# A three-layer graph convolution on one core: nine dense tiles in layer 0 instead of eight, and a new order for the end of that layer

## The reference, cut to what matters

```python
def _gcn_conv(x, W, b, src, dst, norm, n_nodes):
    xw = x @ W
    msg = xw[src] * norm[:, None]
    out = jax.ops.segment_sum(msg, dst, num_segments=n_nodes)
    return out + b
...
src, dst, norm = _gcn_norm(edge_index, n)     # 6250 nodes, 106250 edges sorted by dst, then self loops again
h = _gcn_conv(x, W1, b1, src, dst, norm, n)
h = _gcn_conv(h, W2, b2, src, dst, norm, n)
h = _gcn_conv(h, W3, b3, src, dst, norm, n)
return _layernorm(x + h, axis=-1)
```

## Time and profile before

| | us |
|---|---|
| median of 3 runs | 2347.21 (2343.35 to 2349.53) |
| the profiled execution's own time | 2344.56 |
| its span | 2342.7 |
| PE busy | 2024.8 (86%) |
| POOL busy | 1611.0 (69%) |
| DVE busy | 1490.5 (64%) |
| ACT busy | 803.4 (34%) |

### The profile page before, as it was taken

How to read it: one execution, slowest core, us unless ns; L and a number is a source line. 1 busy time by engine, 2 the same in 40 slices (tenths; PEclk the granted TensorE clock), 3 DMA queues, 4 the chain that set the end, 5 groups by cost and what they waited for, 6 DMA issues and landing times.

```text
span 2342.7 us, 32832 instructions
## 1 busy us (share of the span) xinstructions
PE 2024.8 (86%) x10242; PEld 1157.4 (49%) x10242; DVE 1490.5 (64%) x3665; ACT 803.4 (34%) x1521; POOL 1611.0 (69%) x1698
## 2 busy tenths in 40 slices
PE   6655777899989988779999999998899999999764
PEld 6321223454445433246666566664466666666431
DVE  8435776777767764355555555556656666666787
ACT  0602553444434433233333333334333333323110
POOL 0257777777777777647777777777577777777760
PEclk7766899999999998999999999999899999999876
DMA  8556888888888888758888888889688888898883
GB/s 281 211 167 181 277 271 249 249 251 248 245 254 286 277 253 249 232 159 243 249 248 250 258 269 269 266 264 320 200 242 262 262 260 280 273 287 285 282 279 113
DMA packets 288153, 585.68 MB, mean 250 GB/s; under 512 B 73204, under 2 KB 132529, under 8 KB 287985
## 3 DMA queue, kind: packets, MB, share of 16 engines
q0 software_dynamic: 132784, 434.04, 60.9%
q1 hardware_dynamic: 155200, 149.59, 19.3%
HBM read 516.40 MB, written 67.06 MB: 249 GB/s over the span
## 4 chain that ended last, share of the span: by engine, by line
PE 34%; POOL 12%; issue 6%; DVE 2%; DMA 2%; ACT 0%; DVEq 0%; ACTq 0%
PE ps L1299 25%; POOL ring L972 12%; PE ps L1186 7%; PE ps L1197 1%; DMA ring<-y_dram,kept 1%; PE ps L1198 1%; DVE acc L2115 0%; PE ps L1354 0%; DVE ln L1973 0%; DMA out_dram<-row_sb 0%; DVE acc L1918 0%; DMA onehot<-a_dram 0%; DVEq L1914 0%; DVE y_words L1964 0%; DVE y_words L1971 0%
## 5 line engine op out<-in xcount | busy, mean ns | idle before, releaser
L972 POOL DMA_INDIRECT ring<-y_dram,kept x1650 | 1582.4, 959 | 588.0 <-issue 492.3
L1186 PE MATMUL ps<-ring,onehot 128*32 128x512 f32 x3300 | 467.7, 634 | 80.0 <-DMA ring<-y_dram,kept 78.7
L2115 DVE SCALAR_TENSOR_TENSOR acc<-ps,acc 128x512 f32<-128x512 f32 x494 | 341.1, 690 | 277.7 <-PE ps L1299 261.6
L1299 PE MATMUL ps<-dense_first,wide_a 128*128 128x512 f32 x1144 | 321.3, 402 | 14.0 <-DVE dense_first L2086 6.4
L1299 PEld LDWEIGHTS ps<-dense_first,wide_a 128*128 128x128 f32 x1144 | 213.8, 191 | 103.7 <-issue 26.7
L1299 PE MATMUL ps<-dense_next,wide_a 128*128 128x512 f32 x820 | 238.6, 399 | 8.0 <-ACT wide_a L1542 6.7
L1542 ACT CAST wide_a<-onehot 128x512 fp32r<-128x512 uint8 (+1 forms) x297 | 171.3, 593 | 202.4 <-PE ps L1299 124.2
L1918 DVE SCALAR_TENSOR_TENSOR acc<-ps,mask,acc 128x512 f32 x280 | 197.2, 746 | 67.9 <-issue 65.7
L1299 PE MATMUL ps<-dense_first,y_rows 128*128 128x512 f32 x756 | 211.7, 401 | 2.5 <-DVE dense_next L2086 1.7
L1885 DVE TENSOR_TENSOR onehot<-ps,kept 128x128 f32<-128x128 f32 x417 | 119.4, 287 | 145.6 <-PE ps L1186 143.2
L1503 ACT CAST ring<-ps 128x490 uint8<-128x490 f32 x228 | 154.2, 692 | 138.9 <-PE ps L1256 137.4
(11 more groups left out here) (289 smaller groups left out, 2302.7 us busy)
## 6 DMA issues: line engine op xcount, KB each, us to landing
onehot<-a_dram SPq DMA_DIRECT2D x456, 64.0 KB
ring<-y_dram,kept POOLq DMA_INDIRECT x1650, 4.1
y_dram<-acc SPq DMA_DIRECT2D x99, 256.0 KB, 10.1
a_dram<-ring SPq DMA_DIRECT2D x19, 784.0 KB, 6.0
acc<-in_x_dram SPq DMA_DIRECT2D x1, 12288.0 KB
y_dram<-acc SPq DMA_DIRECT2D x12, 1024.0 KB, 11.0
out_dram<-row_sb SPq DMA_DIRECT2D x48, 256.0 KB
w_sb<-in_x_dram SPq DMA_DIRECT2D x24, 256.0 KB, 4.0
```

Of the source, the lines that this page charges most:

```text
L972: pool.indirect_dma_start(ring[:, s, :], None, y_dram[layer], bass.IndirectOffsetOnAxis(ap=rows, axis=0)).then_inc(done, 16)
L1186: mm = pe.matmul(ps[k * WIDE:(k + 1) * WIDE, g % BANKS, :], wide_hot[:, r, k, :], ring[:, r * CPQ + k, :], start=opens, stop=closes, tile_ ...
L1299: mm = pe.matmul(ps[:, bank, :], wide_slots[n % WIDE_SLOTS][:, P * k:P * (k + 1)], y_parts[(TILES * (layer - 1) + tile) % YSLOTS][:, part, :],
L2115: dve.scalar_tensor_tensor(out=rows, in0=ps[:, UNIT_BANKS[n % len(UNIT_BANKS)], :], scalar=0.5, in1=rows, op0=ALU.mult, op1=ALU.add).then_ ...
```

## The change

`EARLY_DENSE` goes from 8 to 9. One more tile of destinations in layer 0 is then dense, its sparse groups begin one group later, and there are 25 more units. `EARLY_END = 16` sets where the units end, 22 quads ahead of the layer's end instead of 30. The remaining windows end with the units (`REST_QUADS`), before `LATE_AT`. From `LATE_AT` on, finished tiles may come in consecutive quads, and their products go into the bank in which windows were built (`BUILD_BANK`), so that a turn need not wait for the bias of the tile before.

```diff
-EARLY_DENSE = 8
+EARLY_DENSE = 9
+EARLY_END = 16
...
-    REST_QUADS = LAYER_QUADS[0] - REST_AT - 6
...
-    UNITS0_TO = LAYER_QUADS[0] - 6 - 3 * EARLY_DENSE
+    UNITS0_TO = LAYER_QUADS[0] - 6 - EARLY_END
+    REST_QUADS = UNITS0_TO - REST_AT
+    LATE_AT = UNITS0_TO + 2
...
-            at = max(q, at + 2)
+            at = max(q, at + (1 if at >= LATE_AT else 2))
...
+    def late_turn(turn):
+        return FINISH[0][turn][0] >= LATE_AT
...
                 if turn > 0:
                     pe.wait_ge(turn_copied, turn)
-                    pe.wait_ge(h_ready, turn)
+                    if not late_turn(turn - 1):
+                        pe.wait_ge(h_ready, turn)
...
                     for t in finished_at(0, q):
-                        multiply_tile(TURN_OF[0][t], TURN_BANK)
+                        if late_turn(TURN_OF[0][t]):
+                            pe.wait_ge(win_kept, WINDOWS)
+                        multiply_tile(TURN_OF[0][t], BUILD_BANK if late_turn(TURN_OF[0][t]) else TURN_BANK)
...
                     for t in finished_at(0, q):
-                        bias_rows(0, t, h_sb, TURN_BANK, TURN_OF[0][t])
+                        bias_rows(0, t, h_sb, BUILD_BANK if late_turn(TURN_OF[0][t]) else TURN_BANK, TURN_OF[0][t])
```

More of the change, by code:

```diff
@@ L270, in gcn_three_layers_resnorm @@
     assert all(q < LAYER_QUADS[layer] for layer in range(LAYERS) for q, late, t in FINISH[layer])
-    assert all(abs(a[0] - b[0]) > 1 for a, b in zip(FINISH[0], FINISH[0][1:])) and len(pair_of(0)) == PAIR and Y0_SLOTS == 2 * PAIR
+    assert all(b[0] - a[0] > (0 if a[0] >= LATE_AT else 1) for a, b in zip(FINISH[0], FINISH[0][1:])) and window_quad(WINDOWS - 1) < LATE_AT and len(pair_of(0)) == PAIR and Y0_SLOTS == 2 * PAIR
     assert all(len(windows_at(q)) <= WIDE0_SLOTS for q in UNIT0_QUAD) and REST_AT + 2 < UNITS0_FROM and (TILES - 1) % PAIR == 0
```

## The result

| | before | after |
|---|---|---|
| median | 2346.75 us (11 executions, 2341.73 to 2353.21) | 2355.64 us (11 executions, from 2351.85) |
| ratio, 95% interval | | 1.0036 [1.002, 1.0051] |
| the profiled execution, its span | 2344.56, 2342.7 | 2352.24, 2350.4 |

The changed kernel is 0.36% slower, and the interval leaves out 1. The forecast was 2350. One execution of the changed kernel took 10,666.88 us and stays out of the ratio.

The account below looks back on a forecast made before the run. POOL's gathers were taken to bound layer 0, PE only just faster. -15.0 (gathers) + 20 (POOL's waits for PE) - 2 (tail) = +3 us on 2344.6, so 2347.6; the median stands 2.6 higher: 2350, range 2332 to 2368.

Parts of the forecast that it names:

- What bounds the kernel, and the slack: Layer 0: POOL's gathers set the pace, 5.10 us a quad against PE's 4.92; PE may be 16.5 us late unfelt.
- The twelve gathers: Layer 0: three quads fewer take twelve gathers of 1.25 us, 15.0 us, off POOL's chain.
- The price of a third unit at a group's start: Quads beginning a group: a third unit adds 2.7 us; with a second window 6.2, or 4.4 at full clock.
- Third units in third quads: Quads 80 to 111: 1.1 us each, 3.2 with a second window; PE 169.2 us against POOL's 163.2, 6 more.
- Quads 112 to 141: Last stretch with units: PE needs 154.5 us against POOL's 153.0, so POOL waits 1.5 us more.
- most before quad 90, few after 112: Layer 0: where POOL's waits for PE, some 20 us in all, would fall.
- The sum: Whole kernel: 15.0 us saved, 20 us of POOL's waits added, 2 gained in the tail: +3 us.
- PE's waits: Stretch with units: waits for gathered rows fall from 15.2 us to nearly nothing, for DVE and ACT grow from 20 to some 60.
- Finished tiles and tail: End of layer 0: finished tiles in consecutive quads cost 0, the tail gains 2 us, gap to layer 1 about 30.
- a third unit costs 1 us wherever it stands: Rival, quads with units: only 1.0 us per third unit, the slack takes it, 2330 us; faster cases had chance 0.28.
- The low clock: Rival, chance 0.23: stalled quads with three units drop PE's clock, POOL waits 35 us or a little more, 2367 us.
- the 7 us that the prediction called no change: Whole kernel: a difference within 0.3% (7 us) is about what a measurement cannot tell from no change; chance 0.46.

Follow-up runs that it names:

- both edits: Changed kernel, with DVE adding the first of three units before the group and ACT widening the third unit's counts in its own quad: 0.9962, 2695.41 us.
- g0_after: The changed kernel, unedited, run on one of the slower chips: 2713.3 us, ratio 1.0027 to the kernel before on that chip.

## Why the prediction was right, and where it was not

**What bounds the kernel, and the slack: right.** PE's own lengths can be laid beside POOL's 5.10 us a quad, with the starts of the sums of quads 46, 80, 112 and 142 (388.05, 580.17, 749.62, 914.72 us):

| quads | PE, forecast | PE, measured | POOL's need | POOL's wait by that | measured |
|---|---|---|---|---|---|
| 46 to 79 | 199 to 207 | 192.1 | 173.4 | 192.1 - 173.4 - 16.5 = 2.2 | 3.1 |
| 80 to 111 | 169.2 | 169.5 | 163.2 | 6.3 | 6.6 |
| 112 to 141 | 154.5 | 165.1 | 153.0 | 12.1 | 13.0 |

The account with 16.5 us of slack, put together from a chain of gathers, a landing and a sum, holds within 1 us in each stretch once the lengths are the measured ones. Only the first row tests the 16.5: once the slack is used up, POOL goes at PE's pace, and its wait must be the difference of the lengths.

**The twelve gathers: right**, 15.0 us.

**The price of a third unit at a group's start: right, +2.7 (6.34 against 3.64).** With a second window it was +3.9, not 4.4 to 6.2, and quad 46 took 6.27 us, not 9.1. These two make 4.7 of the 7 us and more by which the first stretch came out shorter.

**Third units in third quads: right.** Those that meet a second window took 9.65, 9.53, 9.52 and 9.74 us, priced by 9.79 in the earlier trace rows; those without one 7.72, as in the earlier trace rows.

**Quads 112 to 141: wrong, the step that failed.** "1.5 more" became 13. Quad 112 takes 10.51 us where 4.57 + 1.0 was put, and quad 121 takes 11.12 where 4.57 + 3.2 was: 8.3 us of the 10.6. Another 1.4 are quad 113. Neither part of it was priced: that counts come late (4.19 us in quad 112, none before) and that PE then runs at the low clock ((1 - 0.82) x 5.84 + (1 - 0.81) x 8.05 + (1 - 0.69) x 7.69 = 5.0 us, an estimate, in the three quads). So "most before quad 90, few after 112" was the wrong way round.

**The sum: right by two errors that nearly cancel.** 20 us of waits forecast, 22.7 found, because the first stretch was priced 7 to 15 us too high for PE and the last 11 too low. That the total came so close is luck. The last gather stood 8.3 us later, not 5.

**PE's waits.** For gathered rows 0, as said. For DVE and ACT 26 before, 50 after, not 60. (The prediction's 20 before leave out the 6.3 us that line 1256 waited for DVE's line 2067.)

**Finished tiles and tail: right.** Cost 0; gap 30.5 (30 said), 1.4 us gained of the 2.

**The rivals.** That a third unit costs 1 us wherever it stands is refuted by every quad of 6.09. The low clock did come, but cost hardly more than before. By (1 - PEclk) x PE busy, an estimate, it took 9.2 us in eight of the changed kernel's quads with units (46, 54, 55, 112, 113, 121, 139 and 140) and 8.6 us in six of before (43, 61, 101, 105, 106 and 124), where that rival had 18 more. What changed is where it fell: 6.4 us of it in the last stretch, in which POOL had no slack left. The Trainium skill, TensorE: Matmul & The Clock Gate, "A second HAM failure mode: psum-queue depth-cycling", has it where small idles between groups of products come often: at a group's start the trace agrees in the quad at 436.89 (0.83) and disagrees at 533.52 and 550.67 (1.00), so the rule alone does not say where the clock falls.

**From 2350 to 2355.6.** The profiled execution came out at 2352.24, 4.6 above the sum of 2347.6: 2.7 from POOL's waits, 0.9 from longer gathers, 0.6 from the gap, the rest from layers 1 and 2 (1.5 longer) less 0.9 ahead of the first gather and behind the last. Its median stands 3.4 above it, where 2.6 were put. Together they carry it just past the 7 us that the prediction called no change.

**What stays open.** Why gathers took a little longer. Why the counts of quad 112 landed late: of the suspects, the order against the y rows is ruled out, and the store of a tile of A was not moved by any run. What the crowded windows cost on the first chip, and whether both edits help there: its PE waited 49.8 us, and no run of them was made on it. Nine tiles with the old end of the layer did not run either, so no experiment parts the ninth tile from the new end.

## What to carry to other kernels

When an engine with 3.5% of slack (4.92 us a quad against 5.10) gets more work, don't price the work but the places: add up its length stretch by stretch against the other engine's, subtract the depth of the ring once, and look for the places where it must wait for a third engine's turn in an in-order list. Price also what the added work needs to have loaded, since a late load costs the full time once the slack is used up. And a stall is often cheaper to move than to outrun: here two reorderings of a few lines gave 18 us on one of the slower chips, more than the 15.0 of the gathers left out. And when one change does two things, as this one moves units and crowds windows, run each alone: eight tiles with the new end lost more than the whole change.

## What the runs showed of the hardware

The same kernel takes 2347 us on one chip and 2706 to 2742 on four others. Its gathers are issued as fast there: the row of line 977 in `after` and in `g0_after` (number, ns min/median/max, first and last start):

```profile
L977 POOL DMA_INDIRECT ring<-y_dram,kept x1638: 940/946/2167, 137.3 to 2306.9; - x182
...
  PE ps L1191: 53.3, 35
```

```profile
L977 POOL DMA_INDIRECT ring<-y_dram,kept x1638: 940/946/2211, 137.2 to 2670.1; - x182
...
  remote: 235.4, 115
  PE ps L1191: 218.3, 87
```

946 ns in both. What grows is the waiting: 453.7 us for PE and "remote" where the first chip has 53.3. Of these 400.4 us more, 46.9 only take the place of the usual pauses (440.4 us of them instead of 487.3), and the gaps between layers are 11.0 longer: 364.5 us, where the spans differ by 363.7. Waits put down to "issue", of up to 5.7 us on PE, appear with it. What makes them longer on those chips no run here shows.
